# A four-layer graph network: when GpSimd issues its gathers and its 4-byte scatters in the first stage

## The reference

```python
diff = x[dst] - x[src]                                    # layer 0
max_diff = segment_max(diff, dst); max_diff = where(isneginf(max_diff), 0, max_diff)
L0 = relu(concatenate([x, max_diff], 1) @ W + b)

x1 = swish(x @ lin_W.T + lin_b)                           # layer 1
agg1 = segment_sum(f1 * x1[src], dst); agg2 = segment_sum(f2 * x1[src], dst)
h1 = swish((agg1 @ rel1.T + b + x1 @ root1.T) @ lin1.T + b1)      # h2 in the same way
h = concatenate([h1, h2], 1) @ cat_W.T + cat_b + x1
for i in range(3): h = swish(h @ lins_W[i].T + lins_b[i]) + h
L1 = graph_norm(h) @ final_W.T + final_b                  # over all nodes

L2 = relu(segment_sum((x @ W)[src] * norm, dst) + b)      # with self loops
L3 = relu(layernorm(segment_sum((x @ W)[src] * w, dst) + b) * gamma + beta)
```

## Time and profile before

| | |
|---|---|
| median of 3 runs | 5741.66 us |
| runs | 5741.35 to 5745.12 us |
| span of the profiled execution | 6600.4 us |
| stage nodes01, first to last L897 | 38.2 to 2479.7 us |
| PE busy over the span | 5017.6 us (76%) |
| POOL busy over the span | 4147.3 us (63%) |

### The profile page before, as it was taken

The page is one execution under the profiler, slowest core; times in us unless marked ns, Lnnn a source line. Parts: engine busy times, 40 slices in busy tenths (PEclk is TensorE's granted clock), DMA queues, the critical chain, the costliest instruction groups (busy, mean ns, idle before and its releaser), DMA issues. The chain is left out here.

```text
span 6600.4 us, 83361 instructions
## 1 busy us (share of the span) xinstructions
PE 5017.6 (76%) x20419; PEld 3024.6 (46%) x20419; DVE 4068.7 (62%) x7765; ACT 3374.9 (51%) x8245; POOL 4147.3 (63%) x4026
## 2 busy tenths in 40 slices
PE   6888888888888886999999989999688842222222
PEld 4554545444544452444444457777466632222211
DVE  4554555555555553877777789999766654444444
ACT  4655666656656663444444457777544532222222
POOL 6555556555555655666666448888766646666666
PEclk9999999999999998999999999999865555555555
DMA  3323333332333332555555479999755532222221
GB/s 101 111 91 102 95 104 103 95 103 93 105 102 95 105 97 75 172 156 156 156 153 154 148 267 391 391 388 383 274 157 157 155 90 67 68 69 68 68 67 57
DMA packets 471012, 955.80 MB, mean 145 GB/s; under 512 B 118095, under 2 KB 187771, under 8 KB 470809
## 3 DMA queue, kind: packets, MB, share of 16 engines
q1 hardware_dynamic: 365448, 802.80, 36.1%
q0 software_dynamic: 100352, 149.23, 8.7%
q10 hardware_dynamic: 5008, 1.60, 0.1%
HBM read 571.40 MB, written 387.38 MB: 145 GB/s over the span
## 5 line engine op out<-in xcount | busy, mean ns | idle before, releaser
L146 POOL DMA_INDIRECT ring_rows<-t_rows,home_cols x784 | 780.6, 996 | 573.4 <-PE q_ps L186 236.5
L186 PE MATMUL u_ps_s<-ident,u_weighted 128*128 128x128 f32 x392 | 109.3, 435 | 867.8 <-DVE u_weighted L1920 641.4
L829 DVE TENSOR_TENSOR p_r<-p_s,p_r 128x512 f32<-128x512 f32 x588 | 402.9, 687 | 551.6 <-ACT p_s L762 340.5
L649 POOL TENSOR_TENSOR p_rs<-p_guard,minus_half 128x12 f32<-128x12 f32 (+2 forms) x99 | 242.3, 2447 | 664.6 <-DVE p_guard L897 662.8
L762 ACT ACTIVATE p_s<-p_ps,cols 128x512 f32<-128x512 f32 x588 | 403.0, 685 | 459.2 <-remote 210.6
L153 POOL DMA_INDIRECT out<-u_res,scatter_cols x392 | 405.4, 1034 | 322.4 <-ACT u_res L179 209.6
L146 POOL DMA_INDIRECT u_rows<-t_rows,home_cols x392 | 388.9, 992 | 176.9 <-issue 114.0
L186 PEld LDWEIGHTS u_ps_s<-ident,u_weighted 128*128 128x128 f32 x392 | 70.2, 217 | 896.6 <-DVE u_weighted L1920 545.1
L639 POOL DMA_INDIRECT home<-edge_row_cols,scatter_cols x392 | 395.9, 1010 | 130.4 <-issue 119.1
L146 POOL DMA_INDIRECT p_xs<-in_x,src_cols x392 | 395.6, 1009 | 123.4 <-issue 118.9
L146 POOL DMA_INDIRECT p_xd<-in_x,dst_cols x392 | 404.7, 1032 | 108.8 <-issue 108.8
(11 more groups left out here) (289 smaller groups left out, 14393.9 us busy)
## 6 DMA issues: line engine op xcount, KB each, us to landing
p_x<-in_x SPq DMA_DIRECT2D x98, 512.0 KB
t_rows<-p_o SPq DMA_DIRECT2D x98, 512.0 KB
hT<-p_r SPq DMA_DIRECT2D x98, 512.0 KB
q_hn<-hT SPq DMA_DIRECT2D x98, 512.0 KB
r_h<-hT SPq DMA_DIRECT2D x98, 512.0 KB
r_x<-t_rows SPq DMA_DIRECT2D x98, 512.0 KB
t_rows<-r_y SPq DMA_DIRECT2D x98, 512.0 KB
t_rows<-r_x SPq DMA_DIRECT2D x98, 512.0 KB
```

The costliest lines, as they stand in the source:

```text
L146: nc.gpsimd.indirect_dma_start(out=rows[:, j, :], out_offset=None, in_=table, in_offset=bass.IndirectOffsetOnAxis(ap=idx[:, j:j + 1], axis ...
L649: nc.gpsimd.tensor_tensor(rs[:, q.of(2), lo:hi], guard[:, q.of(2), lo:hi], s["half"][:, lo:hi], ALU.pow).then_inc(rooted, 1)
L829: nc.vector.tensor_tensor(hs[i + 1][:, n.of(4 if i == 2 else 2), :], act_out[i][:, :], hs[i][:, n.of(2), :], ALU.add).then_inc(r_added[i], 1)
```

## The change

POOL's gathers of source rows for block e waited until block e-2 had been transposed (`s_turned`, by PE). They now wait until block e-2 has been scanned (`scanned`, by DVE), the operation that follows. The 4 map scatters of block e had no wait of their own. They now wait for `summed` to reach 2e, which is the sum of node block 2e-1, in the odd step of the pair. Nothing else differs.

```diff
@@ -631,9 +631,10 @@
                     homes(1)
                 e = t
                 if live(e, EB):
-                    after(pool, s_turned, e - 1)
+                    after(pool, scanned, e - 1)
                     if e >= 1:
                         gather(nc, xs[:, e % 2], a["x"], s["src"][:, e * G:(e + 1) * G], xs_in[e % 2])
+                    after(pool, summed, 2 * e)
                     for j in range(G):
                         k = e * G + j
                         nc.gpsimd.indirect_dma_start(
```

## The result

The changed kernel takes 5758.13 us (median of 6 runs, 5754.16 to 5771.83), the kernel before 5743.39 us beside it (6 runs, 5740.49 to 5748.64). The ratio is 1.0027, interval 1.0017 to 1.0037: slower by 15 us. That is a quarter of a per cent, small but clear of the spread of the runs. The forecast of no change was wrong; the time lies in its wide range, and the sign is that of the slower rival.

A forecast was written before the change was run, and what follows sets the result against it. PE was the candidate bound, 20.01 us of work in a 24.85 us pair. All terms cost 0, so 5741.66 + 0 = 5742 us (predicted 5741), own range 5730 to 5753, 8-in-10 range 5690 to 5782.

The forecast's parts named there:

- slower rival: Power 0.8 us late on PE's path in half the pairs: 39 us, 5781 us (5820 if all tight); chance 0.26.
- The scatters' 5.07 us fit in: POOL, odd step: without PE waits L897 ends 5.5 us after the sum, leaving room for 5.07 us of scatters.
- Cost: 0: Scatters' wait on POOL: power 0.8 us late in the tight half of pairs, covered before PE, so no cost.
- The start of 0.1 us: POOL: the scatters were to begin 0.1 us behind the odd sum (L858) in every pair.
- The stretch by DVE: Indirect DMA beside two-input DVE work takes 1.46 against 0.95 us; 24 us for slower rival, none in forecast.
- 0.80 us of room against 0.5 us of delay: cost 0: L829 0.5 us late from the late power, PE's L747 0.80 us behind it: PE doesn't see the delay.
- "remote" waits: Waits in the profile not derivable from the program, 208.8 us for one line; PE waits 4.84 us a pair.
- two kinds of pairs: Pairs of 25.7 us (tight, power 0.8 us late) and 23.5 us (power not moved), about half each.
- faster rival: Scatters away from the stores cut remote waits: 106 us profiled, 49 us timed (46% left), 5693 us; chance 0.32.
- The change doesn't do what it says: POOL runs late enough that both waits are already met; scatters move at most 2 us: 5742 us, counted with forecast.
- signs asked for: Forecast: idle before power below about 200 us, some 30 powers released by POOL's queue; slower: L848 wait well above 64.7.
- The gathers' wait and the moved DMA traffic: Source gathers' new wait met 1.2 us earlier, cost 0; scatter traffic moved to the load of x, cost 0.

The follow-up runs named there:

- e1: The kernel before, word for word, profiled again on a chip that gives about 5743 us: 5745.76 us (one run), span 5744.1.
- e12: The changed kernel with two more gathers of 128 rows on POOL ahead of the scatters' wait, where before takes 5743.08 us: 5749.35 us, ratio 1.0005.
- e11: The changed kernel, both waits included, with the scatters held for one node step less (even step's sum of the block before): 5749.53 us, ratio 1.0007.
- e7: The changed kernel with the scatters held longer, until the edge product's bias sum (DVE L877), on a slow chip: 6256.57 us, ratio 0.9587.
- e10: The kernel before, word for word, profiled on the chip where before takes 5743.08 us: 5747.46 us.
- e6: The changed kernel with two small memsets on POOL in passes 4 and 5, on a slow chip (before 6523.98 us): 6121.64 us, ratio 0.9384.
- e8: The kernel before with its map scatters moved behind the power, no new wait, on a slow chip: 6372.13 us, ratio 0.9774.
- e2: The changed kernel without the scatters' wait, so the gathers' wait alone: 5745.51 us against 5743.07, ratio 1.0001.
- e3: The kernel before with only the scatters' wait for the odd sum added; gathers wait for the transpose as before: 5758.66 us, ratio 1.0028.
- e9: The changed kernel once more, on a chip where before takes 5743.08 us: 5753.57 us, ratio 1.0014.
- e5: The changed kernel with two more gathers of 128 rows on POOL in passes 4 and 5, on a slow chip (before 6523.98 us): 6098.98 us, ratio 0.9353.
- e4: The changed kernel with only the last two of the four map scatters waiting for the odd sum: 5746.93 us, ratio 1.0007.
- e14: The kernel before with scatters held until the even step's sum of the block before, gathers' wait included, on a slow chip: 6487.45 us, ratio 0.9795.

## Why the prediction was wrong

**"The scatters' 5.07 us fit in"** is the step that failed. The prediction set 5.5 us from the sum to L897 against 5.07 us of scatters that begin 0.1 us behind the sum. The first number is right: from 1014.13 to 1019.70 it is 5.57 us in e1. The second is not. The start is 0.82 us behind the sum, and the group takes 5.34 us in a usual pair and 6.94 us (1018.20 to 1025.14, where the power begins) in every eighth. 0.82 + 5.34 = 6.16 us are above the 5.65 us at which the guard ends (1038.50 to 1044.15), so the power is late in every pair, not in half of them. With this alone the forecast would still have stood, for the usual pair pays nothing: e12 has the late power in every pair and no hole, and takes 1.0005 of before. What made the cost is a term that the sum doesn't have: in every eighth pair the 1.14 us of the hole and the 0.47 us of the fourth scatter's stretch, of which the prediction's "Cost: 0" for the scatters' wait knows nothing. No row of before shows such a hole.

**The start of 0.1 us** was taken from no row of a waiting indirect DMA. The earlier trace rows show POOL's wait only for a plain power. But the trace of before had the number, in its later stages, of ACT and then of POOL:

```profile
5466.22 1.63 ACT L179 ACTIVATE u_res<-u_v,u_nmB,u_rsB 128x128 f32<-128x128 f32 x4
5468.67 1.01 POOL L153 DMA_INDIRECT out<-u_res,scatter_cols  x1 [11.51 <-ACT u_res L179]
```

ACT ends at 5467.85, and the scatter that waited for it begins 0.82 us later. 25 scatters of this line begin about 0.83 us behind ACT's end, 83 gathers 0.75 us behind PE's modelled end. There are shorter starts too: two gathers of source rows in before begin 0.27 us behind PE's, and the gathers that wait for the scan in e11 0.27 us behind its end, 45 times. What decides between the two wasn't tried, so a range of 0.3 to 0.8 us was the bound that the trace of before gave.

**The stretch by DVE** was seen in the earlier trace rows (1.46 against 0.95 us) and weighed for the slower rival only. It is there in every pair: the first scatter takes 1.46 us, while L830, with two inputs, runs from 1039.22 to 1039.90. The prediction held that it would use up the cover of 0.3 us; it did, together with the start. By that rule of the Trainium skill (GPSIMD Engine Reference, Key points) a shared interface is the cause; the traces agree in place, and the page gives no size. The order of the two starts decides. In the result's trace from 200 to 1900 us, 107 indirect DMAs begin 0.05 to 0.15 us behind the start of L830, L858 or L889, which all have two SBUF inputs, and take 1.46 us in the median; the 72 that begin level with or up to 0.15 us ahead of such an instruction take 0.95 to 0.98 us. In e7, where the scatters begin elsewhere, the first takes 1.01 us. The fourth scatter of the eighth pair, 1.45 us long, begins at 1023.67, just behind L830 at 1023.58.

**"0.80 us of room against 0.5 us of delay: cost 0"** was right in kind and near in size. The room is 0.70 us, and a usual pair pays nothing for a power that is 0.51 us late. The eighth pair, 1.53 us late, pays. The prediction's slower rival had the right place and the right point from which it decides, but its price (0.8 us in half of the pairs, 39 us) was too high: it is 1.09 us in ten pairs, 11 us.

**The profile of before was taken for the timed kernel.** The prediction saw that 859 us of its span weren't in the timed runs, called the "remote" waits the part that it couldn't derive, and then still built on the pair of 24.85 us: the two kinds of pairs, the share of one half, and the faster rival's 46% of waits that should be left in the timed runs. In the traces of before from the two chips that take 5743 us (e1, e10) nothing of them is left.

**The faster rival** has the right sign on the other kind of chip, at several times its price (49 us for the timed runs). Kernels that hold the scatters for the odd sum take 0.935, 0.938 and 0.949 of before there, e7 0.959 with its late power, while the two others that only shift the scatters take 0.977 and 0.980. The changed kernel itself was not run on such a chip; e6 is it but for two memsets. The rival's mechanism, scatters beside the stores that make PE's signals late, was not tried: no run moves the stores, and e8, which takes the scatters out of their old place, keeps 375 us of the "remote" waits.

**"The change doesn't do what it says"** was nearer to the truth than the prediction took it to be. In e1 POOL issues the first scatter 0.24 us ahead of the end of the sum, so there was hardly anything to hold back. But the wait was not yet met, and a wait that holds for some 0.3 us (1038.24, where the last gather ends, to 1038.50) brings the start of 0.82 us with it.

**Of the signs asked for**, the idle before the power did fall below 200 us (16.8), and the scatters do start behind L858 in nearly every pair. The power was released by POOL's own queue in 97 pairs, not 30, and L848's wait rose to 110.0 us from 64.7 and from 73.6 in e1, which the prediction named as the sign of the slower rival, with PE's gap before L748 as the second. Both came.

**The gathers' wait and the moved DMA traffic** cost nothing, as said (e2).

About 11 of the 15 us are accounted for by the ten pairs. That these are the cost rests on the traces of the result, e3 and e9 against e1, e10 and e12; by their times alone e9 and e12 aren't apart. The intervals of e3 and e9 (1.0016 to 1.0039 and 1.0005 to 1.0023) allow for the rest to be the spread between chips and runs. No version here beats both kernels on every chip: where before takes 5743 us nothing beat it, and e12 is level with it; on the slow kind e5, the same kernel as e12, is 6.5% faster than before.

## What to carry to other kernels

When a wait is put in front of POOL's indirect DMAs, add the start behind the semaphore (0.8 us here), the stretch by what DVE does at that moment (0.4 us), and rare pauses of the queue (1.1 us), and ask for the room of the worst pair, not of the mean one. Look for the start in any stage of the trace where such a DMA waits for an engine; it need not be the stage that changes. And see in the run's own trace whether an added wait ever holds: in e4 and e11 it didn't, and then the run says nothing about waits that do. If the profiled span and the timed median differ by more than a few per cent, the waits of the profile may belong to another chip: take the busy times from it, and build no term on its idle times.

## What the runs showed of the hardware

- A POOL indirect DMA that waits for a DVE semaphore begins 0.8 us behind the end of the releasing instruction (1038.50 to 1039.32). In before, scatters of another stage begin 0.83 us behind ACT's end (5467.85 to 5468.67 is one), in e11 gathers 0.27 us behind DVE's scan. Behind its own kind an indirect DMA begins after 0.30 us, and the plain power began 0.09 us behind L897's end in e1.
- An indirect DMA that begins 0.05 to 0.15 us behind the start of a DVE instruction with two SBUF inputs takes 1.46 us in the median (107 in the result's trace); one that begins level with it or up to 0.15 us ahead takes 0.95 to 0.98 us (72).
- In the changed kernel every 96th indirect DMA on POOL's queue begins 1.44 us behind the end of the one before it instead of 0.30. It was there in the result's profile, e3, e6 and e9, in e7 with 1.89 us, and not in e1, e2, e4, e5, e8 or e10 to e14.
- Two of the four chips of the experiments run the kernel before in 6524 and 6619 us, the other two in 5743 us, with runs on each within about 1%. In the traces of the slow ones DVE and ACT wait up to 5.9 us where the profile finds no releaser ("remote"), and the place of a few 4-byte scatters is worth up to 6.5% (e5, with both waits) or 2.3% (e8, the scatters alone).
